# Mixture of experts behind a graph network: the second tile's rows fetched by an indirect DMA instead of gathered by one-hot products

## The chip, the cores and the metric

The kernel runs on one core of a Trainium2 chip. The metric is the device time of one execution in microseconds. The median of three runs of the kernel before is 168.59 us (167.92 to 169.18).

The engines of the core run side by side, each through its own instruction list in order, and wait for each other by semaphores: TensorE (PE in the profile, PEld for its weight loads), VectorE (DVE), ScalarE (ACT), GpSimd (POOL) and SyncE (SP). POOL and SP also issue the DMAs of this kernel.

## What is computed

The input is 625 rows `x` of 256 numbers and 20000 edges. A graph network of three levels (not touched by the change) gives `x1`. The second half sends each row of `x1`, normalised, to the two of eight experts with the best gate scores, and adds both answers to the row:

```python
gate_scores = x @ Wg + bg
_, idx = jax.lax.top_k(gate_scores, K)
mask = jax.nn.one_hot(idx, E, dtype=x.dtype).sum(axis=-2)
...
h = jax.nn.gelu(jnp.einsum('td,edh->teh', xf, W1) + b1[None], approximate=False)
y = jnp.einsum('teh,ehd->ted', h, W2) + b2[None]
out = jnp.einsum('ted,te->td', y, mf)
```

Here t runs over the 625 rows, d over 256 columns, e over 8 experts, h over 512 hidden columns, and K is 2.

## The kernel before

The change lies in the second half, the experts' stage. The 1250 pairs of a row and an expert are sorted by expert into slots, each expert's slots are rounded up to whole tiles of 128, and each tile is computed with one expert's weights. Thirteen tiles (`FIXED`) are always computed; a loop behind them takes more if there are more.

A tile s goes through these steps, and the text uses these names:

- **x(s)**: the tile's 128 rows, transposed (columns of x on the partitions), are copied by ACT from a PSUM bank into `xt` (two halves, used in turn).
- **up(s)**: PE multiplies by W1 (4 matmuls of 512 columns, L1675); DVE adds b1 (`add_b1`, L1306); ACT applies gelu (L892).
- **th(s)**: PE transposes the hidden tile (4 pieces, L1688) and ACT copies it to `h_t` (L896).
- **down(s)**: PE multiplies by W2 (8 matmuls, L1694); DVE adds b2 into `y_sb` (`add_b2`, L1310).
- **scatter(s)**: POOL issues an indirect DMA that adds the 128 result rows to `out` (L644). It waits for y(s) and for the whole landing of scatter(s-1).

There are two ways to get a tile's rows. For tiles 0 and 1 DVE builds a matrix of ones and zeros (`hot_slot`, L1276) and PE multiplies the normalised rows `x2_f` with it (20 matmuls, L1668), which gives the transposed tile at once. For the others POOL issues an indirect DMA, **gather(s)**, from the copy `x2_rows` in the chip's main memory into `xg` (L638), and PE transposes what came, **tx(s)** (2 pieces, L1682).

The gathers and scatters need the row number of each slot, `row_of`. DVE makes `slot_i`, `tile_pos`, `in_tile`, `hot_place` and `row_in_tile`; PE multiplies the last two (10 matmuls, L1711, the **row product**); DVE makes `row_of` of the product in four short steps (L1336 to L1341).

The order of all this is written out by hand, engine by engine. PE before: tile 0's one-hot products, up(0), tile 1's one-hot products, th(0), the row product, up(1), down(0), tx(2), and from there a fixed round for s = 1, 2, ...: th(s), up(s+1), tx(s+2), a wait for y(s-1), down(s). POOL before: gather(2), gather(3), gather(4), and then scatter(s) and gather(s+5) in turn (`AHEAD` is 5). DVE adds b1 of tile 1 ahead of b2 of tile 0, and then b1 of tile s+1 ahead of b2 of tile s. The numbers of the experts of the tiles are loaded from `owner_i` into registers of PE and of DVE, two at first and eleven later (`experts_of`).

Of the kernel before, what the change touches and what calls it, by code (L numbers as in the profile page):

```python
# [89 lines left out]
AHEAD = 5  # L90
# [3 lines left out]
def build(nc, x, src, dst, W, B, Wf, bf, Wg, bg, W1, b1, W2, b2, out):  # L94
# [8 lines left out]
    with ctx:  # L103
# [106 lines left out]
        place_1 = sb("place_1", [P, NT], f32, ffn)  # L210
        from_1 = sb("from_1", [P, 2, NT], f32, ffn)
        in_1 = sb("in_1", [P, 2, NT], f32, ffn)
# [15 lines left out]
        hot_slot = sb("hot_slot", [P, 2, NT, P], f32, ffn)  # L228
# [173 lines left out]
        def gather_ps(h):  # L402
            return (bank[0], g_ps[1])[h][:, 0:D].rearrange("p (k s) -> p k s", k=KC)
# [119 lines left out]
        def _(pool):  # L523
# [123 lines left out]

            for s in range(2, AHEAD):
                gather(s, row_of[:, s:s + 1])
# [24 lines left out]
        def _(act):  # L674
# [223 lines left out]
            def x_gathered(h):  # L898
                act.wait_ge(gathered, h + 1)
                act.copy(xt[:, :, h * P:(h + 1) * P], gather_ps(h)).then_inc(xt_ready, 1)  # L900
# [23 lines left out]
        def _(dve):  # L924
# [349 lines left out]
            def one_hot(h, place, a, b):  # L1274

                dve.tensor_tensor(hot_slot[:, h, a:b, :], iota_p[:].unsqueeze(1).broadcast_to((P, b - a, P)),  # L1276
                                  place[:, a:b].unsqueeze(2).broadcast_to((P, b - a, P)), ALU.is_equal)\
                    .then_inc(hot_ready, 1)

            one_hot(0, place_0, 0, 3)  # L1280
            one_hot(0, place_0, 3, NT)
# [26 lines left out]
            def add_b2(s, b, e):  # L1308
# [5 lines left out]
            wait_marked()  # L1314
# [47 lines left out]
        def _(pe):  # L1362
# [299 lines left out]
            def gather(h):  # L1662

                for t in range(NT):
                    if t in (0, 3):
                        pe.wait_ge(hot_ready, 3 if h else 1 + t // 3)
# [92 lines left out]
```

## Time and profile before

| | us |
|---|---|
| median of three runs | 168.59 |
| the profiled execution, its own time | 168.71 |
| its span, first to last instruction | 166.6 |
| PE busy (matmul) | 142.3 (85% of the span) |
| PE weight loads | 120.0 (72%) |
| DVE busy | 88.4 (53%) |
| ACT busy | 65.6 (39%) |
| POOL busy | 63.6 (38%) |

The profiled execution is 2.1 us longer than its span; that part lies around the first and the last instruction. The experts' stage begins at about 97 us of the span. The profile follows the chain of work that ended last back from the end; a line of it has the start, the length, and either an engine with the tile it wrote and its line, a DMA, or "issue" (the engine waited for nothing that the profile shows). Two times that touch in the chain are work and what released it. "Idle before" in a timeline row is how long the engine had stood, and what ended that.

### The profile page before, as it was taken

What the parts mean: (1) busy time and instruction counts of PE and PEld (TensorE: products, weight loads), DVE (VectorE), ACT (ScalarE), POOL (GpSimd) and SP (SyncE); (2) the same over time, 40 slices, a digit from 0 to 9 for tenths busy, and PEclk for the clock granted to TensorE, in tenths of its full rate; (3) what the DMA queues carried; (4) which work ended last, traced back from release to release, by engine and by line L of the source; (5) the groups of instructions that cost most, each with busy time, mean ns of one, the idle gap of its engine ahead of it and who ended that gap; (6) DMA issues with size and microseconds to landing.
All of it is one profiled execution on the core that took longest, in us unless ns stands there. A gap on an engine that the chain in (4) does not pass through costs nothing.

```text
span 166.6 us, 2975 instructions
## 1 busy us (share of the span) xinstructions
PE 142.3 (85%) x988; PEld 120.0 (72%) x989; DVE 88.4 (53%) x246; ACT 65.6 (39%) x187; POOL 63.6 (38%) x78
## 2 busy tenths in 40 slices
PE   1433789998999999999999989889999999999720
PEld 1322569988999999999999877556666666667510
DVE  6799999789299951381158894222222222222210
ACT  7527894686270312140214631233333333333200
POOL 5805030000377199910002000273666666634431
PEclk9999999999999999999999999999999999999995
DMA  4969999998004897100001450033344433322232
GB/s 126 292 202 382 366 366 276 163 325 299 29 6 116 276 292 280 57 4 0 0 4 59 128 189 4 0 94 63 65 63 67 63 63 63 63 31 35 31 31 31
DMA packets 16871, 20.85 MB, mean 125 GB/s; under 512 B 1778, under 2 KB 13300, under 8 KB 16724
## 3 DMA queue, kind: packets, MB, share of 16 engines
q1 hardware_dynamic: 13796, 16.79, 31.1%
q0 software_dynamic: 3056, 3.80, 15.6%
q8 instruction: 12, 0.20, 0.5%
q14 instruction: 7, 0.06, 0.1%
HBM read 17.33 MB, written 3.26 MB: 124 GB/s over the span
## 4 chain that ended last, share of the span: by engine, by line
PE 70%; DVE 17%; issue 4%; DMA 3%; ACT 2%; POOL 1%; ACTq 0%; POOLq 0%; DVEq 0%
PE cnt_ps L1694 13%; PE bank L1675 8%; PE g_ps L1675 5%; PE cnt_ps L1503 5%; PE bank L1503 4%; PE cnt_ps L1688 4%; DVE hot_lo L980 3%; PE g_ps L1422 3%; PE g_ps L1366 3%; PE bank L1422 2%; PE g_ps L1367 2%; PE g_ps L1368 2%; PE cnt_ps L1366 2%; PE cnt_ps L1367 2%; PE cnt_ps L1368 2%
## 5 line engine op out<-in xcount | busy, mean ns | idle before, releaser
L644 POOL DMA_INDIRECT out_rows<-y_sb,row_of x13 | 20.6, 1584 | 21.3 <-DMA out_rows<-y_sb,row_of 18.6
L1694 PE MATMUL cnt_ps<-w_sb,h_t 128*128 x104 | 24.7, 380 | 0.9 <-ACT h_t L896 0.9
L1694 PEld LDWEIGHTS cnt_ps<-w_sb,h_t 128*128 128x128 f32 x104 | 18.9, 190 | 4.1 <-issue 2.1
L638 POOL DMA_INDIRECT xg<-x_rows,row_of x11 | 10.9, 994 | 18.8 <-DVE row_of L1341 15.7
L1310 DVE TENSOR_TENSOR y_sb<-cnt_ps,b_bc 128x256 f32<-128x256 f32 x13 | 5.5, 424 | 17.5 <-PE cnt_ps L1694 17.5
L980 DVE TENSOR_TENSOR hot_lo<-iota_lo,edge_rel 125x1024 bf16<-125x1024 int16 x20 | 13.7, 686 | 1.1 <-PE g_ps L1422 1.1
L1675 PE MATMUL bank<-w_sb,xt 128*128 x28 | 13.4, 600 | 0.7 <-ACT xt L900 0.6
L1422 PE MATMUL bank<-hot_key,hot_lo 125*128 125x45 bf16 (+4 forms) x80 | 8.4, 244 | 5.5 <-DVE hot_key L983 4.1
L892 ACT ACTIVATE h_act<-h_pre 128x512 f32<-128x512 f32 x13 | 8.2, 630 | 10.8 <-DVE h_pre L1306 10.8
L1306 DVE TENSOR_TENSOR h_pre<-bank,b_bc 128x512 f32<-128x512 f32 x7 | 4.8, 691 | 13.8 <-PE bank L1675 13.8
L896 ACT COPY h_t<-cnt_ps 128x512 f32<-128x512 f32 x13 | 7.6, 585 | 10.1 <-PE cnt_ps L1688 10.1
L1675 PE MATMUL g_ps<-w_sb,xt 128*128 x24 | 11.4, 596 | 0.0
L1422 PEld LDWEIGHTS bank<-hot_key,hot_lo 125*128 125x128 bf16 x80 | 5.2, 124 | 8.0 <-DVE hot_key L983 5.7
L1422 PE MATMUL g_ps<-hot_key,hot_lo 125*128 125x45 bf16 (+4 forms) x80 | 8.5, 245 | 2.0 <-DVE hot_key L983 1.8
L887 ACT COPY xt<-bank 128x256 f32<-128x256 f32 x11 | 4.1, 372 | 15.1 <-PE bank L1682 15.1
L598 POOL TENSOR_TENSOR w_stage<-w_stage 128x512 f32<-128x512 f32 x1 | 1.3, 1293 | 21.9 <-DMA w_stage<-in_L_gnn_Wf 21.9
L1306 DVE TENSOR_TENSOR h_pre<-g_ps,b_bc 128x512 f32<-128x512 f32 x6 | 4.1, 692 | 10.0 <-PE g_ps L1675 10.0
L1503 PE MATMUL bank<-a_hi,ys_hi 128*128 128x384 f32 (+1 forms) x30 | 9.1, 317 | 0.0
L1503 PE MATMUL bank<-a_hi,ys_lo 128*128 128x384 f32 (+1 forms) x30 | 9.0, 316 | 0.0
L746 ACT CAST ys_hi<-ys_f 128x256 fp32r<-128x256 f32 x10 | 4.1, 406 | 12.5 <-DVE ys_f L1067 12.5
L983 DVE TENSOR_TENSOR hot_key<-key_tables,edge_rel 125x360 bf16<-125x360 int16 (+4 forms) x20 | 8.9, 443 | 0.0
L1171 DVE SCALAR_TENSOR_TENSOR ut_lo<-bank,ut_hi 128x384 fp32r<-128x384 f32 x4 | 2.2, 558 | 12.4 <-ACT ut_hi L866 12.4
(283 smaller groups left out, 396.3 us busy)
## 6 DMA issues: line engine op xcount, KB each, us to landing
w_sb<-in_L_ffn_W SPq DMA_DIRECT2D x16, 512.0 KB, 8.7
b_bc<-in_L_ffn_b SPq DMA_DIRECT2D x8, 256.0 KB, 4.7
w_stage<-in_L_gnn_W SPq DMA_DIRECT2D x3, 512.0 KB, 4.9
w_stage<-in_L_gnn_Wf SPq DMA_DIRECT2D x4, 256.0 KB, 5.7
b_bc<-in_L_ffn_b SPq DMA_DIRECT2D x1, 1024.0 KB, 8.9
x_sb<-in_L_gnn_bf POOLq DMA_DIRECT2D x1, 640.0 KB, 15.1
x_rows<-x_f SPq DMA_DIRECT2D x1, 640.0 KB, 3.4
x_sb<-in_x SPq DMA_DIRECT2D x1, 512.0 KB
```

The costliest lines, as they stand in the source:

```text
L638: pool.indirect_dma_start(out=xg[:, b, :], out_offset=None, in_=x2_rows, in_offset=bass.IndirectOffsetOnAxis(ap=rows, axis=0)).then_inc(x_ ...
L644: pool.indirect_dma_start(out=out, out_offset=bass.IndirectOffsetOnAxis(ap=rows, axis=0), in_=y_sb[:, b, :], in_offset=None, compute_op=AL ...
L892: act.activation(h_act[:, h, :], h_pre[:, h, :], ACT.Gelu).then_inc(act_ready, 1)
L896: act.copy(h_t[:], bank[2].rearrange("p (k s) -> p k s", k=HC)).then_inc(h_t_ready, 1)
L980: dve.tensor_tensor(hot_lo[:, u % RING:u % RING + 2, :, :], iota_lo[0:EP].unsqueeze(1).broadcast_to((EP, 2, P, CT)), rel[:, 0].unsqueeze(2 ...
L983: dve.tensor_tensor(hot_keys(u, 2), turn_keys(u // UNROLL)[0:EP].rearrange("p n w i -> p (n w) i").unsqueeze(1) .broadcast_to((EP, 2, NT * ...
L1306: dve.tensor_tensor(h_pre[:, h, :], up_bank(h)[:, :], b1_bc[:, ds(e, 1), :], ALU.add).then_inc(pre_ready, 1)
L1366: pe.matmul(out_, lh, rh, start=first, stop=False, skip_group_check=True)
L1422: last = pe.matmul(pane(k), hot_lo[:, u % RING, :, i], hot_keys(u)[:, 0, :, i], start=i == i0, stop=i == i0 + n_i - 1, skip_group_check=True)
L1503: step = pe.matmul(o, y[:, u, m], a_t[:, u, cols], start=first and u == 0 and y is y_parts[0], stop=u == NT - 1 and y is y_parts[-1], skip ...
L1675: last = pe.matmul(up_bank(h)[:, :], xt[:, k, h * P:(h + 1) * P], w1_sb[:, ds(e, 1), k, :], start=k == 0, stop=k == KC - 1)
L1694: last = pe.matmul(bank[3][:, 0:D], h_t[:, k, :], w2_sb[:, ds(e, 1), k, :], start=k == 0, stop=k == HC - 1)
```

## The change

- Tile 1's rows come by gather(1) and tx(1), as those of the later tiles. Its one-hot matrix on DVE with the five steps for it (`from_1`, `in_1`, `place_1` and the second `one_hot`) and its 20 matmuls on PE are gone, and ACT copies x(1) from the same PSUM bank as the later tiles.
- DVE makes the whole of `row_in_tile` ahead of `add_b1` of tile 0; before, the larger part came behind it.
- PE does the row product right behind up(0), ahead of th(0). up(1) moves behind down(0), with tx(1) ahead of it.
- POOL issues gather(1), gather(2), gather(3), and then scatter(s) and gather(s+4) in turn (`AHEAD` is 4): three gathers ahead of the first scatter as before, but each of them one tile lower.

```diff
-AHEAD = 5
+AHEAD = 4
...
-            for s in range(2, AHEAD):
+            for s in range(1, AHEAD):
                 gather(s, row_of[:, s:s + 1])
...
             def x_transposed(s, h):
-                act.wait_ge(x_t_done, s - 1)
+                act.wait_ge(x_t_done, s)
...
-            x_gathered(0)
+            act.wait_ge(gathered, 1)
+            act.copy(xt[:, :, 0:P], gather_ps).then_inc(xt_ready, 1)
             gelu(0, 0)
-            x_gathered(1)
             h_transposed(0)
+            x_transposed(1, 1)
             gelu(1, 1)
             x_transposed(2, 0)
...
-            mark(dve.tensor_scalar(from_1[:], slot_1[:], float(P), None, ALU.subtract))
+            mark(dve.tensor_scalar(slot_i[:], slot_1[:], float(P - 1), None, ALU.add))
             wait_marked()
             dve.tensor_copy(owner_i[:], owner[:]).then_inc(experts_ready, 1)
-            mark(dve.scalar_tensor_tensor(in_1[:], from_1[:], float(P), from_1[:], ALU.is_le, ALU.mult))
-            wait_marked()
-            chain(dve.tensor_tensor(place_1[:], in_1[:, 0, :], in_1[:, 1, :], ALU.max))
-            mark(dve.tensor_scalar(slot_i[:], slot_1[:], float(P - 1), None, ALU.add))
-            one_hot(1, place_1, 0, NT)
...
-            dve.wait_ge(b1_in, 16 * EXPERTS)
-            add_b1(0, 0, e_of[0])
...
+            dve.wait_ge(experts_ready, 1)
+            e_of = experts_of(mybir.EngineType.DVE, 0, 2)
+            dve.wait_ge(b1_in, 16 * EXPERTS)
+            add_b1(0, 0, e_of[0])
             e_of = e_of + experts_of(mybir.EngineType.DVE, 2, FIXED)
             dve.wait_ge(row_ps, 1)
...
-            gather(0)
+            gather_first()
             pe.wait_ge(experts_ready, 1)
             e_of = experts_of(mybir.EngineType.PE, 0, 2)
             up(0, 0, e_of[0])
-            gather(1)
             e_of = e_of + experts_of(mybir.EngineType.PE, 2, FIXED)
-            transpose_h(0, 0)
...
             last.then_inc(row_ps, 1)
-            up(1, 1, e_of[1])
+            transpose_h(0, 0)
...
                 down(s, e_of[s])
                 if s == 0:
+                    transpose_x(1, 1)
+                    up(1, 1, e_of[1])
                     transpose_x(2, 1)
```

PE's list from up(0) on, before (L1675 is up, L1668 the one-hot products, L1688 th, L1711 the row product, L1694 down; `TENSOR_LOAD` is the load of the experts' numbers):

```order
L1675 MATMUL bank<-w_sb,xt 128x512
L1668 MATMUL g_ps<-hot_slot,x_f 128x128 x10
L410 TENSOR_LOAD owner_i
L1688 MATMUL cnt_ps<-ident,h_act 128x128 x4
L1711 MATMUL bank<-row_in_tile,hot_place 128x36 x10
L1675 ISA
L1675 MATMUL g_ps<-w_sb,xt 128x512
L1675 ISA
L1675 MATMUL g_ps<-w_sb,xt 128x512
L1694 REGISTER_ALU
L1694 MATMUL cnt_ps<-w_sb,h_t 128x256
```

The one-hot products of tile 1, th(0), the row product and up(1) all stand between up(0) and down(0). The same place in the changed kernel (L1662 is up, L1696 the row product, L1675 th, L1681 down, L1669 tx):

```order
L1662 MATMUL bank<-w_sb,xt 128x512
L406 TENSOR_LOAD owner_i
L1696 MATMUL bank<-row_in_tile,hot_place 128x36 x10
L1675 MATMUL cnt_ps<-ident,h_act 128x128 x4
L1681 REGISTER_ALU
L1681 MATMUL cnt_ps<-w_sb,h_t 128x256
...
L1669 MATMUL bank<-ident,xg 128x128 x2
L1662 ISA
L1662 MATMUL g_ps<-w_sb,xt 128x512
L1662 ISA
L1662 MATMUL g_ps<-w_sb,xt 128x512
L1669 MATMUL bank<-ident,xg 128x128 x2
L1675 MATMUL cnt_ps<-ident,h_act 128x128 x4
```

The row product now follows up(0) at once, only th(0) is left between it and down(0), and up(1) stands between tx(1) and tx(2), with th(1) right behind.

DVE's list around the row numbers, before (L1306 is `add_b1`, L1336 the first step to `row_of`):

```order
L1318 CAST tile_pos<-tile_pos_i 128x20
L1306 ISA
L1306 TENSOR_TENSOR h_pre<-bank,b_bc 128x512
L1322 TENSOR_TENSOR in_tile<-tile_pos,tile_no 128x180
L1325 TENSOR_TENSOR hot_place<-iota_pos,tile_pos 128x1280
L1330 TENSOR_TENSOR row_in_tile<-in_tile,row_part 128x360
L410 TENSOR_LOAD owner_i
L1336 TENSOR_SCALAR row_high<-bank 128x18
```

And in the changed kernel (L1310 is `add_b1`):

```order
L1293 CAST tile_pos<-tile_pos_i 128x20
L1295 TENSOR_TENSOR in_tile<-tile_pos,tile_no 128x180
L1298 TENSOR_TENSOR hot_place<-iota_pos,tile_pos 128x1280
L1303 TENSOR_TENSOR row_in_tile<-in_tile,row_part 128x360
L406 TENSOR_LOAD owner_i
L1310 ISA
L1310 TENSOR_TENSOR h_pre<-bank,b_bc 128x512
L406 TENSOR_LOAD owner_i
L1323 TENSOR_SCALAR row_high<-bank 128x18
```

The three steps of the row pairs have moved ahead of `add_b1` of tile 0; the load of eleven experts' numbers still stands between that addition and the first step to `row_of`.

## Rows read from the trace of the kernel before

**Rows 1.** Chain of waits at the stage's start: start us, length us, what.

```profile
100.09 1.98 PE bank L1675 x4
102.07 2.23 PE g_ps L1668 x20
104.30 0.55 issue
104.85 0.63 PE cnt_ps L1688 x4
105.48 0.57 PE bank L1711 x10
...
106.83 0.28 issue
107.11 2.91 DMA xg<-x_rows,row_of
...
110.06 0.44 PE bank L1682 x2
...
111.05 1.98 PE bank L1675 x4
```

**Rows 2.** Chain of waits in one round of the middle and at the end.

```profile
129.66 1.73 PE cnt_ps L1694 x8
131.39 0.44 PE cnt_ps L1688 x4
131.83 1.72 PE g_ps L1675 x4
133.54 0.22 PE bank L1682 x2
...
156.38 0.59 ACT h_t L896
...
157.29 1.98 PE cnt_ps L1694 x8
```

**Rows 3.** Two stretches: length; busy PE, PEld, DVE, ACT, POOL; clock; DMA share; GB/s.

```profile
100.00:111.05 11.05, 9.81 (x57) 6.95 (x57) 3.98 (x12) 2.67 (x6) 3.03 (x4) 1.00 0.09 25
...
115.25:152.18 36.93, 36.93 (x165) 25.55 (x163) 9.97 (x19) 14.29 (x27) 21.19 (x16) 1.00 0.38 57
```

**Rows 4.** Timeline of DVE and ACT around the row numbers: start, length, instruction.

```profile
100.08 0.17 DVE L1318 CAST tile_pos<-tile_pos_i 128x20 bf16<-128x20 int32 x1
...
102.30 0.69 DVE L1306 TENSOR_TENSOR h_pre<-bank,b_bc 128x512 f32<-128x512 f32 x1 [2.05 <-PE bank L1675]
...
103.03 0.63 ACT L892 ACTIVATE h_act<-h_pre 128x512 f32<-128x512 f32 x1 [3.08 <-DVE h_pre L1306]
...
103.90 0.38 DVE L1330 TENSOR_TENSOR row_in_tile<-in_tile,row_part 128x360 bf16<-128x360 bf16 x1
...
106.07 0.18 DVE L1336 TENSOR_SCALAR row_high<-bank 128x18 f32<-128x18 f32 x1 [1.80 <-PE bank L1711]
```

**Rows 5.** Timeline of results, scatters and gathers on DVE and POOL.

```profile
115.12 0.42 DVE L1310 TENSOR_TENSOR y_sb<-cnt_ps,b_bc 128x256 f32<-128x256 f32 x1 [1.19 <-PE cnt_ps L1694]
...
116.35 1.59 POOL L644 DMA_INDIRECT out_rows<-y_sb,row_of  x1 [2.36 <-DVE y_sb L1310]
...
131.60 0.42 DVE L1310 TENSOR_TENSOR y_sb<-cnt_ps,b_bc 128x256 f32<-128x256 f32 x1 [1.26 <-PE cnt_ps L1694]
...
132.83 1.59 POOL L644 DMA_INDIRECT out_rows<-y_sb,row_of  x1 [1.22 <-DMA out_rows<-y_sb,row_of]
...
134.72 0.99 POOL L638 DMA_INDIRECT xg<-x_rows,row_of  x1 [0.30 <-issue]
```

**Rows 6.** Issue to landing: first the 11 gathers into xg, then the transfers to out_rows.

```profile
DMA to landing us min/median/max: 2.7/2.8/3.0
...
DMA to landing us min/median/max: 3.7/3.8/3.9
```

**Rows 7.** Page, DMA issues: tile, size, median us from issue to landing.

```profile
x_rows<-x_f SPq DMA_DIRECT2D x1, 640.0 KB, 3.4
```

More of the change, by code:

```diff
@@ L209, in build @@
         place_0 = sb("place_0", [P, NT], f32, ffn)
-        place_1 = sb("place_1", [P, NT], f32, ffn)
-        from_1 = sb("from_1", [P, 2, NT], f32, ffn)
-        in_1 = sb("in_1", [P, 2, NT], f32, ffn)
         in_tile = sb("in_tile", [P, 2, SLOT_TILES, NT], bf16, ffn)
@@ L227, in build @@
         iota_p = sb("iota_p", [P, P], f32, ffn)
-        hot_slot = sb("hot_slot", [P, 2, NT, P], f32, ffn)
+        hot_slot = sb("hot_slot", [P, NT, P], f32, ffn)
         x2_f = sb("x2_f", [P, NT, D], f32, ffn)
@@ L400, in build @@
         COLS = [slice(0, SPLIT), slice(SPLIT, NPAD)]
-        def gather_ps(h):
-            return (bank[0], g_ps[1])[h][:, 0:D].rearrange("p (k s) -> p k s", k=KC)
+        gather_ps = bank[0][:, 0:D].rearrange("p (k s) -> p k s", k=KC)
         def rest_of_tiles(eng, least=0):
@@ L1272, in _, with one_hot @@
             chain(dve.tensor_reduce(place_0[:], slot[:], AX.X, ALU.min))
-            def one_hot(h, place, a, b):
-                dve.tensor_tensor(hot_slot[:, h, a:b, :], iota_p[:].unsqueeze(1).broadcast_to((P, b - a, P)),
-                                  place[:, a:b].unsqueeze(2).broadcast_to((P, b - a, P)), ALU.is_equal)\
+            def one_hot(a, b):
+                dve.tensor_tensor(hot_slot[:, a:b, :], iota_p[:].unsqueeze(1).broadcast_to((P, b - a, P)),
+                                  place_0[:, a:b].unsqueeze(2).broadcast_to((P, b - a, P)), ALU.is_equal)\
                     .then_inc(hot_ready, 1)
-            one_hot(0, place_0, 0, 3)
-            one_hot(0, place_0, 3, NT)
+            one_hot(0, 3)
+            one_hot(3, NT)
             spread_e = (1, SLOT_TILES, EXPERTS)
@@ L1293, in _ @@
             mark(dve.tensor_scalar(owner[:, SLOT_TILES:], owner[:, SLOT_TILES:], 0.0, None, ALU.max))
-            mark(dve.tensor_scalar(from_1[:], slot_1[:], float(P), None, ALU.subtract))
+            mark(dve.tensor_scalar(slot_i[:], slot_1[:], float(P - 1), None, ALU.add))
             wait_marked()
             dve.tensor_copy(owner_i[:], owner[:]).then_inc(experts_ready, 1)
-            mark(dve.scalar_tensor_tensor(in_1[:], from_1[:], float(P), from_1[:], ALU.is_le, ALU.mult))
-            wait_marked()
-            chain(dve.tensor_tensor(place_1[:], in_1[:, 0, :], in_1[:, 1, :], ALU.max))
-            mark(dve.tensor_scalar(slot_i[:], slot_1[:], float(P - 1), None, ALU.add))
-            one_hot(1, place_1, 0, NT)
-            def add_b1(s, h, e):
-                dve.wait_ge(up_done, s + 1)
-                dve.tensor_tensor(h_pre[:, h, :], up_bank(h)[:, :], b1_bc[:, ds(e, 1), :], ALU.add).then_inc(pre_ready, 1)
-            def add_b2(s, b, e):
-                dve.wait_ge(down_done, s + 1)
-                dve.tensor_tensor(y_sb[:, b, :], bank[3][:, 0:D], b2_bc[:, ds(e, 1), :], ALU.add).then_inc(y_ready, 1)
-            dve.wait_ge(experts_ready, 1)
-            e_of = experts_of(mybir.EngineType.DVE, 0, 2)
-            wait_marked()
             mark(dve.tensor_single_scalar(tile_pos_i[:, 0], slot_i[:], 7, ALU.arith_shift_right))
@@ L1332, in _, with add_b1, add_b2 @@
                               row_part[:].unsqueeze(2).broadcast_to(parts_of), ALU.mult).then_inc(row_pairs_ready, 1)
+            def add_b1(s, h, e):
+                dve.wait_ge(up_done, s + 1)
+                dve.tensor_tensor(h_pre[:, h, :], up_bank(h)[:, :], b1_bc[:, ds(e, 1), :], ALU.add).then_inc(pre_ready, 1)
+            def add_b2(s, b, e):
+                dve.wait_ge(down_done, s + 1)
+                dve.tensor_tensor(y_sb[:, b, :], bank[3][:, 0:D], b2_bc[:, ds(e, 1), :], ALU.add).then_inc(y_ready, 1)
+            dve.wait_ge(experts_ready, 1)
+            e_of = experts_of(mybir.EngineType.DVE, 0, 2)
+            dve.wait_ge(b1_in, 16 * EXPERTS)
+            add_b1(0, 0, e_of[0])
             e_of = e_of + experts_of(mybir.EngineType.DVE, 2, FIXED)
@@ L1659, in _, with gather_first @@
             last.then_inc(prefix_ps, 1)
-            def gather(h):
+            def gather_first():
                 for t in range(NT):
                     if t in (0, 3):
-                        pe.wait_ge(hot_ready, 3 if h else 1 + t // 3)
+                        pe.wait_ge(hot_ready, 1 + t // 3)
                     for k in range(KC):
-                        last = pe.matmul(gather_ps(h)[:, k, :], x2_f[:, t, k * P:(k + 1) * P], hot_slot[:, h, t, :],
+                        last = pe.matmul(gather_ps[:, k, :], x2_f[:, t, k * P:(k + 1) * P], hot_slot[:, t, :],
                                          start=t == 0 and k == 0, stop=t == NT - 1, skip_group_check=True)
```

3 lines of the change are left out of this document (removed).

## The prediction

> **What bounds the kernel now.** I read the chain of waits backwards first. From 111 us on it is PE alone, round after round: down 1.73, th 0.44, up 1.72, tx 0.22 [rows 2], which is 4.11 us a tile. The busy times of the stretch from 115.25 to 152.18 us say the same: PE is busy for all of its 36.93 us, at granted clock 1.00 (2.4 GHz) [rows 3]. So the end of the kernel is fixed by the moment at which this round starts, that is by up(2) at 111.05 us, unless something breaks the round.
>
> The start of the stage is different. Between 100.00 and 111.05 us PE is busy for 9.81 us [rows 3], and the chain there goes up(0), one-hot products of tile 1, th(0), row product, row numbers, 2.91 us of waiting for gather(2), tx(2), th(1), up(2) [rows 1]. The one-hot products are on the chain, but so is the way to the row numbers, and up(1) and down(0) are hidden beside the row numbers and the gather.
>
> The third thing is POOL's round, read from the timeline: a scatter takes 1.59 us to issue, the gather behind it starts 1.89 us after the scatter's start (132.83 to 134.72) [rows 5], gathers land 2.7 to 3.0 us after their start and scatters 3.7 to 3.9 [rows 6]. As each scatter waits for the landing of the one before and then 0.3 us, POOL's own round is 4.1 us too, hidden by a hair.
>
> **The change part by part.**
>
> *What leaves.* On PE 20 one-hot matmuls, 2.23 us on the chain [rows 1]. What leaves DVE lies beside PE's up(0), where DVE waited 2.05 us for PE anyway [rows 4]: worth nothing by itself.
>
> *Row numbers sooner.* The three steps of the row pairs took from the end of add_b1 (102.30 + 0.69 = 102.99) to 103.90 + 0.38 = 104.28, 1.29 us. Started behind tile_pos (100.25 at the latest) they end by 101.6, before up(0) does at 102.07. So the row product waits only for up(0) and the load of the experts' numbers, for which I take the 0.55 us of issue that stood there: 102.07 + 0.55 + 0.57 = 103.2. DVE then still has add_b1 of tile 0 (until 102.99) and its own load of eleven numbers ahead of row_high. No row shows that load alone: it is nothing at least, and at most the time from 104.28 to row_high at 106.07, 1.79 us. I take PE's 0.55, the same load on another engine: row_high at 103.55. The four steps and the issue took 107.11 - 106.07 = 1.04 us, so gather(1) starts at 104.6 (104.3 to 105.8), where gather(2) started at 107.11. The rows come 2.5 us sooner. It lands 2.91 us later, at 107.5 (107.2 to 108.7). The store of x2_rows takes 3.4 us [rows 7]; x2 is whole before up(0), so it has landed by 103.5.
>
> *Tile 0 on PE.* gelu ends at 103.03 + 0.63 = 103.66 [rows 4]; th(0) follows with 0.63 to 104.3; the copy of h_t costs 157.29 - 156.38 = 0.91 [rows 2]; down(0) takes 1.98 and ends at 107.25. gather(1) lands 0.25 us later, so PE waits a little: this part is nearly even, and rows that came sooner still would be worth a quarter of a microsecond.
>
> *Tile 1, now on the path.* tx(1) 0.44 from 107.54 (landing and 0.04), 0.55 for the copy of x and the start of up (110.50 to 111.05 in rows 1), up(1) 1.98, add_b1 0.23 + 0.69, gelu 0.04 + 0.63, then th(1) 0.05 + 0.57. That is 5.2 us behind 107.54: up(2) at 112.7. Between up(1) and th(1) PE has only tx(2), 0.22 us, to do; before, down(0) and the wait for gather(2) lay there and cost nothing more. DVE's add_b1 of tile 1 still stands ahead of add_b2 of tile 0, so y(0) now waits for up(1) and comes at about 111.8, and with it scatter(0) at 112.6; gather(4) behind it lands at 117.4, in time for tx(4) at 118.5. up(2) before started with its weights unloaded (1.98 against 1.72), which this order hides, 0.26 us. So the round starts 112.7 - 111.05 - 0.26 = **1.4 us later**. Bounds: with the load on DVE free, a transposition of 0.22 and up(1) at 1.72, 0.7 us; with the load at 1.79, 2.6 us.
>
> *The gathers one tile closer.* tx(s+2) now needs the gather behind scatter(s-2), not s-3. The new ring is: end of tx, down 1.73, y 0.63 (131.39 to 132.02), 0.81 to the scatter (115.54 to 116.35, and 132.02 to 132.83), 1.89 to the gather, 2.85 to land (between the median and the upper end), 0.04 and an unhidden tx 0.44: 8.39 us for two tiles, where PE needs 2 x 4.11 = 8.22. The ring is a little longer than PE's two rounds. tx(4) has a slack of 1.1 us, tx(5) none; from there four pairs of tiles are left, each 0.14 to 0.17 us longer: **0.6 us**. With landings of 2.7 us it is nothing; with 3.0 it is 0.32 a pair, 1.3 us. POOL's own 4.1 us round does not add to it.
>
> The Trainium skill (DMA: Bandwidth & Descriptors, Anatomy of one DMA — SWDGE (gpsimd) path) fits a DMA issued by GpSimd as 2.0 us plus its bytes over 436 GB/s, by our estimate 2.3 us for the 128 KiB of a tile. The trace says 2.7 to 3.0 [rows 6]. By the page the ring would be 7.8 us, with no stall, and the sum 0.6 us less; I go by the rows.
>
> *The sum.* 168.71 (the profiled execution) + 1.4 + 0.6 = 170.7. That execution lies 0.12 above the median of the runs, so against the median 168.59 I forecast **170.5 us**, 1.1% slower.
>
> **The rivals.**
>
> *A free ring.* The start costs 0.7 to 1.4 us and the gathers still come in time (2.7 us to land): 169.3 to 170.0. For it: all 11 gathers of before landed in 2.7 to 3.0 us, most of them right behind a scatter as they will be now. Against it: the lower end is needed, in every round.
>
> *A slow start or a slow ring.* DVE's load costs over a microsecond, or landings stretch to 3.0 us: 171.2 to 172.0. Against it: PE's load of the same numbers showed 0.55.
>
> *PE's work sets the time (faster).* PE is the chain from 111 us on and loses 2.23 us of matmuls against a tx(1) of 0.22. If the new gaps at the start were no larger than the old ones, 11.05 - 9.81 = 1.24 us [rows 3], the time would be 168.6 - 2.0 = 166.6. It decides if th(1) ends by 109.0 instead of 112.7. Against it: gelu(1) has to lie between up(1) and th(1), and PE's list has nothing to put there; the gaps as worked out above (load 0.55, th(0) 0.5, h_t 0.9, tx(1) 0.3, up(1) 0.55, gelu(1) 1.4) add up to over 4 us. The Trainium skill (Perfetto Trace Analysis, Identifying the Most-Contended Engine) says to optimise the engine with the highest occupancy first, and for TensorE to judge by weight loads rather than by matmul busy time. By that rule, less work on PE would give this rival's time; the trace bears it out from 111 us on and not at the start, where weight loads fill 6.95 of 11.05 us [rows 3].
>
> *No net change.* The start costs nothing because PE's gaps and the sooner rows cancel: 168.6. It needs up(2) at 111.05, which the path of tile 1 does not allow by 0.7 us even at its lower bounds.
>
> **How the numbers follow.** About 1%, 1.7 us, is what a measurement of this kernel can tell from no change, so slower begins at 170.3. The forecast (169.9 to 171.1) gets 0.55, the free ring 0.23, the slow start or ring 0.14, PE's work 0.06, no net change 0.02. Three quarters of the forecast's case lies over 170.3: slower 0.41 + 0.14 = 0.55. Same 0.14 + 0.23 + 0.02 = 0.39. Faster 0.06. The range leaves out PE's work, no change and the ends of the others: 169.4 to 171.9.
>
> **What would show each step right or wrong.** Right: row_of about 2.5 us sooner; gather(1) at about 104.6; PE standing for over a microsecond ahead of th(1); up(2) at 112.4 to 112.7; waits of PE for DMA at tx(5), tx(7) and so on of 0.1 to 0.3 us, and a mean round of 4.15 to 4.2 us where it was 4.11. Wrong: th(1) before 111 us; a round of 4.11 as before (the ring is free); rounds above 4.3 us or landings above 3.0 us (the gathers and scatters disturb each other more than before); a granted clock under 1.00 ahead of up(2), where it was 1.00 [rows 3], since PE stands more there.

## The result and the profile after

The changed kernel takes **173.53 us** (median of four runs, 172.69 to 174.19), the kernel before in the same comparison 168.82 us: 1.031 times as long, with a 95% interval of 1.027 to 1.034. It is slower, as forecast, but by 4.7 us where 1.9 were forecast, and the time lies above the range. The intervals below leave out single executions at a lower granted clock (of 1.2, 1.3, 1.6 and 4.1, some 1.7 to 3 us longer than the others, and three of the kernel before, one of 246.7 us), so a part of what the clock costs is not in them; the medians and the times in brackets hold them.

The span of the profiled execution is 172.0 us; the execution took 174.19 us, the longest of the four. To find where the time went I cut the stage into three pieces at moments that PE's and POOL's timelines show in every kernel: the **start**, from the first instruction of up(0) to that of th(2); the **rounds**, from th(2) to th(12); and the **end**, from th(12) to the start of the last scatter.

| us | up(0) at | start | rounds | end |
|---|---|---|---|---|
| before | 100.09 | 14.72 | 40.87 | 5.74 |
| after | 101.31 | 17.46 | 41.80 | 6.34 |
| difference | 1.22 | 2.74 | 0.93 | 0.60 |

The four differences add up to 5.49, which is the distance of the two profiled executions (174.19 - 168.71 = 5.48). The first of them lies ahead of the changed code: up(0) began between 99.37 and 101.31 us in the kernels of this study, and this execution is the latest of them. Forecast were 1.4 for the start, 0.6 for the rounds and nothing for the end.

The chain of waits of the changed kernel from up(0) to up(2) (start us, length us, what; L1662 is up, L1669 tx, L1675 th, L1310 `add_b1`, DVEq the issue queue of DVE):

```profile
101.31 1.99 PE bank L1662 x4
...
103.52 0.69 DVE h_pre L1310
104.21 1.85 DVEq L406
...
106.11 0.18 DVE row_high L1323
...
106.86 0.28 issue
107.15 2.89 DMA xg<-x_rows,row_of
...
110.08 0.45 PE bank L1669 x2
...
111.07 1.99 PE g_ps L1662 x4
...
113.20 0.70 DVE h_pre L1310
...
113.92 0.64 ACT h_act L888
...
114.61 0.66 PE cnt_ps L1675 x4
115.26 1.72 PE bank L1662 x4
```

The shape is the forecast one: tile 1 is on the path with its gather, its transposition, up, bias, gelu and th(1), and up(2) then runs at 1.72 with its weights hidden [rows 1]. One line was not forecast at this size: behind `add_b1` of tile 0, **the chain stands on DVE's queue for 1.85 us at line 406**, the load of the eleven experts' numbers, before `row_high` may start. These 1.85 us are the part that `add_b1` does not cover; the trace lists the loads of DVE themselves (count: shortest, median, longest in ns, first to last start; of two loads the median is the mean), and the long one, of 2.51 us, begins at 103.6:

```profile
L406 DVEq TENSOR_LOAD <-owner_i x2: 546/1528/2509, 100.7 to 103.6; - x2
```

Where before the chain went through the one-hot products, th(0) and the row product, and that load lay beside them, it is now on the path.

PE's and PEld's waits of the changed kernel from 100 to 165 us (what waited, for what: us in total, times, longest):

```profile
PE bank L1669 <- DMA xg<-x_rows,row_of: 2.1, 2, 1.8
...
PEld bank L1669 <- DMA xg<-x_rows,row_of: 7.6, 9, 2.2
```

The longest pair, 1.8 and 2.2, is tx(1) waiting for gather(1); the other eight of PEld, 5.4 us, are the tx of the rounds. Before, PEld waited for that DMA once:

```profile
PEld bank L1682 <- DMA xg<-x_rows,row_of: 0.9, 1, 0.9
```

POOL's timeline shows the end (start, length, instruction, idle before it and what ended it; L640 is the scatter):

```profile
154.04 1.59 POOL L640 DMA_INDIRECT out_rows<-y_sb,row_of  x1 [1.22 <-DMA out_rows<-y_sb,row_of]
158.77 1.58 POOL L640 DMA_INDIRECT out_rows<-y_sb,row_of  x1 [3.15 <-DMA out_rows<-y_sb,row_of]
162.76 1.56 POOL L640 DMA_INDIRECT out_rows<-y_sb,row_of  x1 [2.40 <-DMA out_rows<-y_sb,row_of]
166.91 1.56 POOL L640 DMA_INDIRECT out_rows<-y_sb,row_of  x1 [2.59 <-DMA out_rows<-y_sb,row_of]
```

Scatter(9), at 154.04, was followed only 4.73 us later (in the kernel before, the steps from the second scatter on are 4.02 to 4.18), and the last three scatters wait for one another's landing. The line of landings explains it, with 3.9 as the longest before [rows 6]:

```profile
DMA to landing us min/median/max: 3.7/3.8/4.5
```

### The profile page after: what moved, and what is told of

It reads as the page before. It is cut to its first block, busy times and chain, and to the rows that moved or that the text cites. A ratio compares the mean times of both kernels' runs of the same rounds, so it can differ in the third digit from the quotient of the medians.

```text
span 172.0 us, 2936 instructions
## 1 busy us (share of the span) xinstructions
PE 142.1 (83%) x970; PEld 117.5 (68%) x971; DVE 87.7 (51%) x242; ACT 65.5 (38%) x187; POOL 65.0 (38%) x79
## 3 DMA queue, kind: packets, MB, share of 16 engines
HBM read 17.46 MB, written 3.26 MB: 120 GB/s over the span
## 4 chain that ended last, share of the span: by engine, by line
PE 70%; DVE 12%; issue 5%; DMA 5%; ACT 3%; POOL 2%; DVEq 1%; ACTq 0%; POOLq 0%
PE cnt_ps L1681 11%; PE bank L1662 6%; PE bank L1490 5%; PE g_ps L1662 5%; PE cnt_ps L1490 5%; DMA xg<-x_rows,row_of 3%; PE g_ps L1354 3%; PE g_ps L1353 3%; PE g_ps L1355 3%; PE cnt_ps L1675 3%; DVE hot_lo L973 3%; PE g_ps L1409 3%; PE bank L1409 2%; PE cnt_ps L1353 2%; PE bank L1353 2%
## 5 line engine op out<-in xcount | busy, mean ns | idle before, releaser
L640 POOL DMA_INDIRECT out_rows<-y_sb,row_of x13 | 20.6, 1588 | 25.4 <-DMA out_rows<-y_sb,row_of 17.1
L1681 PE MATMUL cnt_ps<-w_sb,h_t 128*128 x104 | 24.7, 381 | 1.6 <-ACT h_t L892 1.6
L1681 PEld LDWEIGHTS cnt_ps<-w_sb,h_t 128*128 128x128 f32 x104 | 18.8, 190 | 4.5 <-issue 2.5
L634 POOL DMA_INDIRECT xg<-x_rows,row_of x12 | 12.0, 997 | 17.9 <-DVE row_of L1328 14.6
L1662 PE MATMUL bank<-w_sb,xt 128*128 x28 | 13.3, 596 | 0.6 <-ACT xt L895 0.6
L1662 PE MATMUL g_ps<-w_sb,xt 128*128 x24 | 11.4, 597 | 0.5 <-ACT xt L883 0.5
L1310 DVE TENSOR_TENSOR h_pre<-bank,b_bc 128x512 f32<-128x512 f32 x7 | 4.8, 692 | 13.6 <-PE bank L1662 13.6
L1310 DVE TENSOR_TENSOR h_pre<-g_ps,b_bc 128x512 f32<-128x512 f32 x6 | 4.2, 692 | 14.8 <-PE g_ps L1662 14.8
L1669 PEld LDWEIGHTS bank<-ident,xg 128*128 128x128 f32 x24 | 2.9, 140 | 9.3 <-DMA xg<-x_rows,row_of 7.6
L1675 PE MATMUL cnt_ps<-ident,h_act 128*128 128x128 f32 x52 | 8.0, 276 | 1.4 <-ACT h_act L888 1.3
```

Of the source, the lines that this page charges most:

```text
L634: pool.indirect_dma_start(out=xg[:, b, :], out_offset=None, in_=x2_rows, in_offset=bass.IndirectOffsetOnAxis(ap=rows, axis=0)).then_inc(x_ ...
L640: pool.indirect_dma_start(out=out, out_offset=bass.IndirectOffsetOnAxis(ap=rows, axis=0), in_=y_sb[:, b, :], in_offset=None, compute_op=AL ...
L1310: dve.tensor_tensor(h_pre[:, h, :], up_bank(h)[:, :], b1_bc[:, ds(e, 1), :], ALU.add).then_inc(pre_ready, 1)
L1662: last = pe.matmul(up_bank(h)[:, :], xt[:, k, h * P:(h + 1) * P], w1_sb[:, ds(e, 1), k, :], start=k == 0, stop=k == KC - 1)
L1675: last = pe.transpose(bank[2][:, k * P:(k + 1) * P], h_act[:, h, k * P:(k + 1) * P], ident[:])
L1681: last = pe.matmul(bank[3][:, 0:D], h_t[:, k, :], w2_sb[:, ds(e, 1), k, :], start=k == 0, stop=k == HC - 1)
```

## The experiments

Four causes were to be told apart: the **load** (its length on DVE, and on PE ahead of the row product), the **ring** (the gathers one tile closer to their scatter), the **clock** of PE, which the new gaps might let fall, and **tile 1's own path**. "Before" is the median of the kernel before on the chip of that comparison: 168.61 for 1.1 to 1.4, 169.12 for 1.5, 1.6, 3.1 and 3.2, 168.55 for 2.1 to 2.4, 168.57 for 4.1 to 4.3. A profile is always of one execution only. Brackets hold the 95% interval of the ratio to it.

### 1. Taking the changed kernel's costs away

**1.1 DVE's load behind `row_of`.**

```diff
             add_b1(0, 0, e_of[0])
-            e_of = e_of + experts_of(mybir.EngineType.DVE, 2, FIXED)
...
             dve.tensor_tensor(row_of[:], row_1[:], unused[:], ALU.add).then_inc(rows_ready, 1)
+            e_of = e_of + experts_of(mybir.EngineType.DVE, 2, FIXED)
```

> Theory L (the load of eleven experts' numbers on DVE, 1.85 us of the changed kernel's chain between add_b1 of tile 0 and row_high, makes the row numbers late): with the load behind row_of, row_high starts when the row product ends, 104.9 in the changed kernel's trace instead of 106.1, so gather(1), tx(1) and up(2) come 1.2 us sooner and the time is about 172.3 us against the changed kernel's 173.5. Rival S (PE's new order with tile 1 on the path sets the start, whatever the row numbers do): row_of may come sooner, but tx(1) does not by more than 0.2 us, and the time stays at 173.5.

Measured: 172.96 us (171.86 to 173.13), 1.024 [1.019 to 1.030]. The start took 16.26 instead of 17.46. The chain shows what became the limit, PE's own load of the eleven numbers, which stands between up(0) and the row product:

```profile
100.46 1.98 PE bank L1662 x4
102.44 0.87 issue
103.31 0.77 PE bank L1696 x10
...
104.11 0.18 DVE row_high L1322
```

The row product ended at up(0) + 3.62, and DVE began `row_high` at once. So DVE's load cost 1.2 us of the start, and PE's showed 0.87 where the prediction had 0.55. Of the time little came back: 4.35 us over before, where the changed kernel stands 4.71 over. The rounds took 42.29 in this profile, 0.5 more than after, which takes part of the gain.

**1.2 Four gathers ahead** (`AHEAD` 4 to 5 in the changed kernel, so gather(1) to gather(4) before the first scatter).

> The changed kernel with gather(1) to gather(4) ahead of the first scatter, so that each later gather is a tile earlier again. Theory R (gathers that are one tile closer make PE wait for rows, stretch the rounds by 0.09 us and delay the last scatter): PE no longer waits for a DMA at tx(5) and later, the mean round from th(2) to th(12) falls from 4.17 to 4.10 us, and the time is 172.0 to 172.6 us. Rival N (the longer rounds and the late last scatter are scatters that happened to land slowly in that one execution): the time stays at 173.5. The start does not change by either.

Measured: 172.25 us (171.06 to 174.58), 1.020 [1.014 to 1.026]. The profile is of the longest execution, 174.58. The rounds took 40.87, to the hundredth what they took before, and PE waits for no gather in them. The start however took 19.96. The stretches of 2 us show why (length; busy time of PE, PEld, DVE, ACT, POOL; granted clock; DMA share; GB/s):

```profile
108.00:110.00 2.00, 0.44 (x2) 0.20 (x2) 0.00 (x0) 0.27 (x1) 1.67 (x2) 1.00 0.43 129
110.00:112.00 2.00, 1.76 (x4) 0.78 (x5) 0.00 (x0) 0.10 (x1) 0.95 (x1) 0.83 0.28 82
112.00:114.00 2.00, 1.39 (x4) 0.37 (x2) 0.88 (x2) 0.16 (x1) 0.00 (x0) 0.50 0.16 51
114.00:116.00 2.00, 1.47 (x5) 1.25 (x6) 0.14 (x1) 1.06 (x3) 1.02 (x1) 0.50 0.00 0
116.00:118.00 2.00, 2.00 (x4) 0.67 (x3) 0.00 (x0) 0.26 (x1) 1.62 (x2) 0.50 0.45 41
```

Behind a stretch in which PE did almost nothing, waiting for gather(1), the granted clock fell to 0.50 (1.2 GHz) for some 6 us, and up(1), th(1) and up(2) took 2.74, 1.11 and 3.04 instead of 1.99, 0.66 and 1.72. Without these 2.52 us the start would be 17.44, that of the changed kernel.

**1.3 Both loads late** (1.1, and PE's load moved from behind up(0) to behind up(1)).

> As the kernel with DVE's load behind row_of, and PE's load of the same eleven numbers moved from ahead of the row product to behind up(1), where PE waits for gelu(1). Theory L: the row product starts at the end of up(0), row_high right behind add_b1 of tile 0, row_of 1.9 us sooner than in the changed kernel; tx(1) is then bound by the end of down(0) and comes 1.7 us sooner: 171.8 us. If PE's load takes over a microsecond behind up(1), a part of that comes back. Rival S: 173.5.

Measured: 171.69 us (170.20 to 174.03), 1.024 [1.014 to 1.033], too wide to rank it against 1.1. Its profile is the execution of 170.20, the shortest of the four: start 15.46, 2.0 us less than after, rounds 41.71. The wait for gather(1) is gone from the chain, and in its place stand tile 0's steps, th(0), the copy of h_t, down(0) and then tx(1): the cover that the prediction had called nearly even.

**1.4 Both loads late, four gathers ahead, and `add_b2` of tile 0 ahead of `add_b1` of tile 1.**

> Both loads late, four gathers ahead of the first scatter, and DVE's add_b2 of tile 0 ahead of add_b1 of tile 1, so that scatter(0) starts about 3 us sooner and the chain of scatters has slack. If the three costs (loads 1.7, ring 0.9, late end 0.6) are separate, the time is 170.3 us. What then remains over the 168.8 of the kernel before, about 1.5 us, is the path of tile 1 (tx(1), up(1), gelu(1) with nothing beside). If theory S or N holds for its part, the time is 171.5 or more. If tile 1's path costs nothing by itself, it is 168.8 or less.

Measured: 170.99 us (169.51 to 171.79), 1.012 [1.004 to 1.020]. Start 17.14, rounds 40.88. The start is longer than in 1.3 because of one line, down(0), at 3.65 where it took 1.97 in 1.6, at granted clock 0.50 from 106 to 108 us:

```profile
105.41 3.65 PE cnt_ps L1682 x8
```

**1.5 A second load of the eleven numbers on DVE** was meant to double the suspected cost.

> The changed kernel with DVE's load of eleven experts' numbers done twice, one behind the other, ahead of row_high. Theory L (one load takes 1.85 us and lies on the path): row_high, gather(1) and up(2) come 1.8 to 1.9 us later, from up(0) to th(2) it takes 19.3 us instead of 17.46, and the time is 175.3 us. If most of the 1.85 us is something that the load only waits for (a start of DVE's sequencer, the row product), a second load adds under 0.6 us: 173.5 to 174.1.

**1.6 Both loads late and four gathers ahead** (1.2 and 1.3 together).

> Both loads late and four gathers ahead of the first scatter, with add_b1 of tile 1 ahead of add_b2 of tile 0 as in the changed kernel. Separates the ring from the first result: if the order of the two additions matters for nothing but the first scatter, the time is that of the kernel with all edits, 170.3 to 171.0 us, with rounds of 4.09 us and no wait of PE for a DMA. If the sooner first scatter was needed for the chain of scatters, the last scatter comes 0.5 us later behind th(12) than there: 171.0 to 171.5.

Measured: 169.90 us (168.90 to 172.14, ten runs), against 169.12: 1.003 [0.999 to 1.007]. Start 15.46, rounds 40.88, end 5.93. With load and ring both gone, the changed way of getting tile 1's rows stands 0.8 us behind before by the medians, and 0.74 by the start. Three of the ten runs took 171.6 to 172.1, at mean granted clocks of 0.973 to 0.984, and the seven others 168.9 to 170.4, five of these at 0.985 to 0.993: which fits a clock that falls in some executions of one and the same program, though 0.984 stands on both sides (171.59 and 168.90).

### 2. The same parts in the kernel before, and the clock held

**2.1 The ring alone** (`AHEAD` 5 to 4 in the kernel before; tile 1 stays one-hot).

> The kernel before with the one edit AHEAD = 4: only gather(2) and gather(3) ahead of the first scatter, so each later gather comes one scatter later, and nothing else changes. Theory R (the ring of result, scatter, gather, transposition is longer than two of PE's rounds): the time from th(2) to th(12) rises from 40.87 to 41.7 us or more and the last scatter comes 0.6 us later behind th(12): 169.8 to 170.4 us. Rival N: the gathers are early enough without the late start, 168.6 us.

Measured: 170.35 us (170.14 to 170.41), 1.010 [1.007 to 1.014]: **with the ring alone the kernel is 1.8 us slower**. Its profile, with a span 1.4 us longer, shows 0.95 of it in the rounds (41.82). PEld's waits for the gathers from 100 to 165 us are

```profile
PEld bank L1682 <- DMA xg<-x_rows,row_of: 6.4, 9, 0.9
```

and half of its rounds have a tx of 0.32 to 0.44 instead of 0.22. The clock was 1.00 through the rounds. Another 0.57 of its longer span is an up(0) that began later, at 100.66, which no part of this edit explains; so the 1.8 us hold more than the profile shows of the ring.

**2.2 The rows sooner alone** (the kernel before with the row pairs ahead of `add_b1`, the row product ahead of the one-hot products, DVE's load behind `row_of`; `AHEAD` stays 5).

```diff
             up(0, 0, e_of[0])
-            gather(1)
-            e_of = e_of + experts_of(mybir.EngineType.PE, 2, FIXED)
-            transpose_h(0, 0)
...
             last.then_inc(row_ps, 1)
+            gather(1)
+            e_of = e_of + experts_of(mybir.EngineType.PE, 2, FIXED)
+            transpose_h(0, 0)
```

> The kernel before, tile 1 still by one-hot products and AHEAD 5, but with the row numbers sooner: DVE makes the row pairs ahead of add_b1 of tile 0, PE does the row product right behind up(0) and the one-hot products of tile 1 after it, and DVE's load of eleven numbers comes behind row_of. Theory T (what makes the start of the changed kernel late is tile 1's path, not the sooner rows): gather(2) starts at about 104.3, PE no longer waits for it ahead of tx(2), and the round starts 0.3 to 0.7 us sooner than in the kernel before: 168.0 to 168.4 us. Rival: the row product ahead of the one-hot products delays up(1) and th(0) by as much as the wait for gather(2) was: 168.6 to 169.2 us.

Measured: 167.74 us (eleven runs, 167.19 to 168.64), 0.995 [0.993 to 0.998], 0.8 us faster than before. Here PE has the one-hot products and tile 1's up to do while the rows come, and the wait for gather(2) is gone.

**2.3 The changed kernel with small products in PE's gaps** (70 of 128x128x128 bf16, none of them used), to hold the clock.

```diff
             up(0, 0, e_of[0])
+            hold(12)
...
             transpose_h(0, 0)
+            hold(10)
...
+                    hold(24)
                     transpose_x(1, 1)
+                    hold(6)
...
                     transpose_x(2, 1)
+                    hold(18)
```

> The changed kernel with 70 small products on TensorE (the kind that the kernel already runs ahead of the routing, 0.06 us each) put into the gaps of its start, into a PSUM bank that nothing reads. Theory K (the new gaps at the start let the granted clock fall to its lower level in some executions: three of the four runs of the changed kernel have a mean clock of 0.976 to 0.979, the kernel before 0.985 to 0.990): every run has a mean clock of 0.983 or more, and the median falls by 0.5 to 1.3 us, to 172.2 to 173.0 us. Rival F (the clock of the start does not matter for the time, or the products only delay what is behind them): the median stays at 173.5 or rises.

Measured: 173.84 us (172.85 to 175.09), 1.032 [1.028 to 1.036]. The granted clock is 1.00 in every stretch from 102 to 118 us and 0.983 to 0.993 in the mean of each run, and the time is that of the changed kernel. So the clock as the main cause fell. It is not shown that the clock costs nothing there. The start of this profile, 17.43, is that of the changed kernel's profile (17.46), whose clock was 1.00 there too, so neither the products nor a clock shows in it, but its rounds took 42.83.

**2.4 Kernel 1.4 with such products** (6, 10, 2, 6 and 18).

> The kernel with late loads, four gathers ahead and the first result sooner, with 42 such products in the gaps of its start. That kernel's profile showed the clock at 0.50 in 106 to 108 us and down(0) at 3.65 us instead of 1.98. Theory K: no such stretch, mean clock 0.985 or more in each run, 169.4 to 169.9 us instead of 170.99. Rival F: 171 or more.

Measured: 170.31 us (169.56 to 170.74), 1.010 [1.007 to 1.013]. Start 16.08, rounds 40.88. Against the profile of 1.4 that is 1.06 less in the start, against 1.6 with its clock at 1.00 it is 0.62 more. That is the products: in the chain eighteen of them take 1.00 us behind PE's late load and ahead of th(1), which comes 2.28 us behind up(1), in 1.6 1.55. Both effects are seen; what the clock is worth can't be read from it to better than that.

### 3. What the sooner rows are worth

**3.1 The kernel before, only DVE's load behind `row_of`.**

> The kernel before with DVE's load of eleven numbers behind row_of and nothing else changed. There the load had from 104.28 to 106.07 us, and the row product ended at 106.05, so a load of 1.85 us and the row product end together. Theory L: row_high stays at the end of the row product, the time is within 0.2 us of 168.55. If the row numbers of the kernel before also waited for the load by more than that: 168.1 or less.

Measured: 169.18 us against 169.12, 1.002 [0.998 to 1.005]: no difference. PE's products and load cover DVE's load there. Its chain shows 2.35 of the load's 2.51 us, and that it now delays `add_b1` of tile 1 (109.35, before 108.00) without harm to the end:

```profile
106.66 0.18 DVE row_of L1340
106.84 2.35 DVEq L410
...
109.35 0.70 DVE h_pre L1306
```

**3.2 Kernel 2.2, and PE loads all thirteen numbers at once, ahead of up(0).**

```diff
-            e_of = experts_of(mybir.EngineType.PE, 0, 2)
+            e_of = experts_of(mybir.EngineType.PE, 0, FIXED)
...
-            e_of = e_of + experts_of(mybir.EngineType.PE, 2, FIXED)
```

> The kernel before with the row numbers sooner (which gave 167.74), and PE's two loads of experts' numbers made one of thirteen numbers ahead of up(0), where PE waits for x(0) anyway. In the kernel with sooner rows the second load stands in the chain with 0.55 us ahead of th(0). If a load of thirteen numbers is hidden behind the one-hot products of tile 0: 167.2 us. If it takes 1.85 us or more as on DVE, it ends after x(0) is there, up(0) starts later, and the time is 167.7 us or above.

Measured: **168.10 us** (twelve runs) against 169.12, 0.9935 [0.991 to 0.996]: the lowest ratio of the study, 1.0 us faster than before, though its interval overlaps those of 2.2 and 4.3. PE has no line of waiting or issue over 0.11 us from up(0) to up(2):

```profile
100.05 1.98 PE bank L1675 x4
102.02 0.55 PE bank L1707 x10
102.58 2.32 PE g_ps L1668 x20
104.90 0.44 PE cnt_ps L1688 x4
105.33 0.11 issue
105.45 1.98 PE g_ps L1675 x4
107.42 1.73 PE cnt_ps L1694 x8
109.15 0.22 PE bank L1682 x2
109.37 0.44 PE cnt_ps L1688 x4
109.81 0.11 issue
109.92 1.98 PE bank L1675 x4
```

### 4. One load in place of two, on both engines

Here PE and DVE each load all thirteen numbers at once, ahead of up(0) and `add_b1` (the edit of 3.2, on both): the cost is taken away and no work is moved behind anything else.

**4.1 In the changed kernel.**

> The changed kernel with one load of all thirteen experts' numbers on PE and on DVE at the place of the load of two, and none of eleven. The trace of the kernel before has the loads as rows: 0.55 us for two numbers, 2.51 (DVE) and 2.65 us (PE) for the eleven from the third on; one load of thirteen on PE took 1.13 us. Theory L2 (the load of eleven is long because of where it starts, and what made the start late was this load): thirteen take 1.1 to 1.2 us on DVE too and are hidden ahead of add_b1 of tile 0; from up(0) to th(2) it takes 15.4 to 15.5 us instead of 17.46, as with both loads late, and the time is 171.2 to 171.8 us. Theory by number (a load costs 0.2 us a number): thirteen take 2.9 us on DVE, add_b1 of tile 0 comes 0.8 us later, the stretch stays above 17 us and the time above 173.

Measured: 170.30 us (169.49 to 172.97), 1.011 [1.007 to 1.014]. That is 1.7 us over before and 3.0 under the changed kernel. The three runs at mean clocks of 0.988 to 0.990 took 169.5 to 170.3, the two at 0.980 and 0.982 took 172.7 and 173.0. The profile is of the execution of 172.65: start 16.99 with down(0) at 3.49 and the clock at 0.50 from 106 to 108 us, rounds 42.13. With down(0) at 1.97 the start would be 15.47.

**4.2 In the changed kernel with four gathers ahead.**

> The same with four gathers ahead of the first scatter. If the loads and the ring are the two terms that the prediction mis-sized, and nothing else is lost, the stretch from up(0) to th(2) is 15.4 to 15.5 us, from th(2) to th(12) 40.9, from there to the last scatter 5.9, and the time is 169.8 us, 0.9 us over the kernel before, which is tile 1's path. If the cause lies elsewhere (the clock, or a slow scatter), the rounds are longer or the time is 170.5 or more.

Measured: 171.45 us (170.97 to 172.53), 1.020 [1.016 to 1.024], a miss. The rounds are 40.87 as they should be; the start is 17.15 where 15.46 would do. It is the same PE list as 1.6 but for the load, with the same busy times ahead (0.94 and 1.24 of the two stretches, there 0.93 and 1.24), and yet the granted clock fell in this profile; the mean clocks of all four runs are low (0.972 to 0.983), so it probably fell in them too. First 4.2, then 1.6, stretches of 2 us:

```profile
102.00:104.00 2.00, 0.94 (x13) 0.81 (x12) 1.27 (x5) 0.63 (x1) 0.00 (x0) 1.00 0.00 0
104.00:106.00 2.00, 1.24 (x6) 0.94 (x6) 0.00 (x0) 0.59 (x1) 1.64 (x2) 0.83 0.09 20
106.00:108.00 2.00, 2.00 (x6) 1.55 (x6) 0.00 (x0) 0.00 (x0) 1.39 (x3) 0.50 0.35 111
108.00:110.00 2.00, 1.45 (x6) 0.89 (x5) 0.00 (x0) 0.37 (x1) 0.94 (x1) 0.82 0.34 92
```

```profile
102.00:104.00 2.00, 0.93 (x14) 0.83 (x13) 1.27 (x5) 0.63 (x1) 0.06 (x1) 1.00 0.00 0
104.00:106.00 2.00, 1.24 (x8) 0.95 (x7) 0.00 (x0) 0.59 (x1) 1.70 (x2) 1.00 0.14 31
106.00:108.00 2.00, 1.45 (x9) 1.00 (x8) 0.00 (x0) 0.37 (x1) 1.39 (x3) 1.00 0.32 100
```

down(0), in the chains of 4.2 and of 1.6:

```profile
105.24 3.65 PE cnt_ps L1680 x8
```

```profile
105.14 1.97 PE cnt_ps L1681 x8
```

That single step is 1.68 us longer, and the whole start 1.69 (17.15 and 15.46). 171.45 less 1.68 is 169.8, 1.2 over before, where 1.6 stands 0.8 over its own before. So the clock is a third cost of this way of starting, of about 1.7 us in an execution that it hits in this place; what lets it fall in one execution and not in the other is not shown.

**4.3 In the kernel before.**

> The kernel before with one load of thirteen numbers on PE and DVE and nothing else changed. The 0.55 us of issue ahead of th(0) in its chain is then gone; the row product, the row numbers and gather(2) come 0.5 us sooner: 168.0 us against 168.55. Tells how much of the gain of the kernel with sooner rows and one load on PE (ratio 0.9935) is the load and how much the order. If the gain there was the order alone: no change.

Measured: 167.92 us (twelve runs, 167.41 to 168.20), 0.996 [0.994 to 0.998], 0.65 us faster. The 0.55 of issue between the one-hot products and th(0) [rows 1] is gone, and gather(2) starts at 106.16 where it started at 107.11; counted from up(0) it is 0.72 sooner, and the start takes 13.89 instead of 14.72.

## Why the prediction was right or wrong

**The step that failed: the load of the eleven numbers on DVE**, in "I take PE's 0.55, the same load on another engine: row_high at 103.55", with 1.79 as the upper bound. Both were read from gaps, and a gap shows only the end of a load that nothing covers, 0.55 behind PE's one-hot products and 1.79 ahead of `row_high`. "No row shows that load alone" was wrong too, since the trace of before lists the loads themselves, among the instructions on `owner_i`:

```profile
L410 PEldq TENSOR_LOAD <-owner_i x2: 556/1600/2645, 98.7 to 102.2; - x2
L410 DVEq TENSOR_LOAD <-owner_i x2: 546/1527/2508, 99.0 to 103.3; - x2
```

The short one on each engine is the load of two numbers; that of eleven takes **2.51 us on DVE and 2.65 on PE**, outside my bounds. That the gap of 0.55 is as long as the short load is chance: PE's long load began at 102.2 and ran beside the one-hot products until 104.85, where th(0) begins [rows 1], and the 0.55 was its tail. DVE's ran from 103.3 to 105.8, covered to its end by PE, whose row product ended at 106.05. The change takes the one-hot products and th(0) away from ahead of the row product. After up(0) ends, `row_high` was forecast 1.48 later (102.07 to 103.55) and came 2.81 later (103.30 to 106.11). The difference, 1.33, is the whole excess of the start: 2.74 measured, 1.4 forecast. 1.1 shows the term by itself, 1.2 us of the start; 1.3 and 1.6 show that with both loads late the start is 15.46, 2.0 less than in the changed kernel.

The rest, point by point.

- **The rows sooner: direction right, size wrong.** From up(0) to `row_high` it now takes 4.80 us where it took 5.98: 1.2 sooner, not 2.5, by the load.
- **Tile 1's path: right.** From gather(1)'s start to up(2) it takes 8.11 us (107.15 to 115.26); forecast was 8.1 (104.6 to 112.7). Each link holds: landing 2.89, tx 0.45, copy and start 0.54, up 1.99, bias and gelu up to th(1) 1.55, th(1) 0.65. PE stands 1.34 us ahead of th(1), as foreseen (1.4), and 1.77 ahead of tx(1), where 0.3 was worked out, because the rows came late by the load.
- **The start at its lower end: right.** With the loads out of the way 1.3 and 1.6 give 15.46, 0.74 over before; the prediction's bound was 0.7.
- **The ring: right in kind and place, and the second term that was mis-sized.** The first rounds that it lengthens are those of tx(5) and tx(7), as forecast, and `AHEAD` 5 takes every such wait away. In this profile the round is 4.18 in the mean (forecast 4.15 to 4.2) and the rounds 0.93 longer. But the seven profiled kernels with `AHEAD` 4 have rounds of 41.71 to 43.05, 0.84 to 2.18 longer than before and 1.4 in the mean, and the medians price the ring at 1.8 us (2.1) and 1.9 (1.2, where the ratio falls from 1.031 to 1.020), uncertain by about 0.5 and 1.2 us: forecast were 0.6, with 1.3 as the bound. With `AHEAD` 5 the rounds are 40.87 or 40.88, in 4.3 41.13. The gathers of the changed kernel kept to 2.7 to 2.9 us; it was single *scatters* that landed late, up to 4.5 us, and the prediction had let scatters vary by nothing.
- **The end: missing.** I had written that POOL's own round of 4.1 us adds nothing. After a late landing it does: the last scatters run behind one another, before too, and the last one started 2.2 us behind its y(12), where it was 1.5 before.
- **The clock: named as what would prove me wrong, priced at nothing.** In the profiled execution it is 1.00 up to up(2), but the three other runs have mean clocks of 0.976 to 0.979, where the kernel before has 0.983 or more in 68 of its 71 executions in the comparisons of the experiments. Where a profile shows it at 0.50 in the start, the steps that it lengthened are the whole excess of the start: without them 1.4, 4.1 and 4.2 come to 15.46 or 15.47, as 1.6 did, and 1.2 and 1.5 to 17.44 and 17.45, as the changed kernel. Its size in the changed kernel's other executions stays open: the run at 0.986 is the longest, at 174.19, and holding the clock (2.3) brought nothing.
- **The rivals.** The slow start came true, at 2.74 beyond even its bound of 2.6, together with the slower ring; each had been given alone. "PE's work sets the time" is refuted: 2.2 us of PE work went and the time rose. By the Trainium skill (Perfetto Trace Analysis, Identifying the Most-Contended Engine) the busiest engine is the one to relieve; here PE's busy time from up(0) to th(2) fell from 13.57 to 12.14 us and that stretch grew by 2.74, because its gaps are set by DVE's queue, a DMA, and the bias and gelu of tile 1.
- **The sum.** 168.71 + 1.4 + 0.6 was the forecast. Of the 2.8 us that are missing at the median, 1.33 is the load by the profile, and up to 1.2 the ring with its late end, by the medians of the experiments 2.1 and 1.2 (in the one execution profiled, rounds and end lie 0.33 and 0.60 over the forecast). How the sum divides in the median execution, and what a fallen clock adds to it, is not settled, since each profile is one execution and up(0) alone moves by 1.9 us between them.

So what was in the change that was good? The rows sooner: with the one-hot products kept, they make the kernel faster by 0.8 us (2.2, start 14.04 where before has 14.72). One load in place of two gives 0.65 without any new order (4.3, start 13.89), and the new order with one load on PE 1.0 (3.2, start 13.63). So both shorten the same wait, and behind the single load the order is worth little more: 0.26 us of start, one profile each. Tile 1's gather costs about 1.8 us against 3.2: 1.6 and 3.2, in one comparison, took 169.9 and 168.1.

## What to carry to other kernels

Read the duration of an instruction where the trace lists it (also those of the issue queues, which count as idle time), not from the gap that it leaves: a gap shows only what its cover does not hide, and a change that removes the cover pays the whole. Work that an engine does "needlessly" while a transfer comes (here 2.2 us of one-hot products) is worth what it hides, and it may keep the engine's clock up, as the unused products of 2.3 and 2.4 did; replace it only by something that is not longer on the chain. A prefetch distance that just fits on medians, with two transfers in a ring that was worked out at 8.39 us against 8.22, has no room for a single late landing.

## What the runs showed of the hardware

- **The length of a register load did not go by its count alone.** Two numbers from the first on took 0.55 us, eleven from the third on 2.51 (DVE) and 2.65 (PE), but thirteen from the first on 1.12 and 1.13. The loads of 4.1 on the same tile:

```profile
L406 PEldq TENSOR_LOAD <-owner_i x1: 1133/1133/1133, 99.4 to 99.4; - x1
L406 DVEq TENSOR_LOAD <-owner_i x1: 1115/1115/1115, 100.1 to 100.1; - x1
```

  The loads of two and of eleven took the same on each engine, to 0.01 us, in every profile that has them. Whether the start decides was not tried.
- **A load runs beside its engine's own instructions and holds up only what stands behind it.** DVE's began at 103.6 in the changed kernel, while `add_b1` ran (103.52 to 104.21), and lay on the chain for 1.85 of its 2.51 us.
- **PE's granted clock fell to 0.50 (1.2 GHz) behind gaps and half-busy stretches of a few microseconds**, and not in each execution: in 4.2 with PE busy for 2.18 of 4 us ahead of it, while 1.6 with 2.17 kept 1.00. It cost 1.35 to 1.7 us where it hit a single step (up(1) at 3.34, down(0) at 3.49 to 3.65).
- **Accumulating scatters landed in 3.7 to 3.9 us before, but single ones in up to 4.5 after and 4.3 in 2.1.** In six of the seven profiles with `AHEAD` 4 the slowest scatter took 4.3 to 4.9 us (the seventh has a gather of 4.1), in the ten with `AHEAD` 5 at most 4.0. Why single ones are late was not found.
